# A recurrent block with an FP4 feed-forward gate: stacked half slices, the pointwise product in two parts, and a new order of work

## The reference

```python
xn = _layernorm(x, axis=-1)
s = _L0_attn_ref(xn, ...)      # the recurrent branch
g = _silu(_L0_ffn_ref(xn, w_gate, w_up, w_down))
return x + s * g

# the recurrent branch (weights of 256 x 256, 512 x 256, 1024 x 256, 256 x 1024)
x = causal_dwconv(rmsnorm(x, conv_norm_g), dw_w, dw_b, pw_w, pw_b) + x   # 3 taps, then pointwise
x = min_gru(rmsnorm(x, gru_norm_g), gru_w) + x                           # a scan along the 512 tokens
h = gelu(rmsnorm(x, ff_norm_g) @ ff_w1.T + ff_b1)
x = h @ ff_w2.T + ff_b2 + x

# the FP4 branch: inner size 704, every operand rounded in blocks of 16
gate, up = fp4_linear(x, w_gate), fp4_linear(x, w_up)
h = silu(gate) * up
h = fp4_linear(h, w_down)
# fp4: scale = max|block| / 6, then the nearest of 0, .5, 1, 1.5, 2, 3, 4, 6
```

## Time and profile before

| | |
|---|---|
| Median of 3 runs | 1086.87 us (1084.11 to 1087.17) |
| The profiled execution's own time | 1085.26 us |
| Its span, first to last instruction | 1083.5 us |
| PE busy | 1061.8 us, 98% of the span |
| DVE busy | 934.5 us, 86% |
| ACT busy | 607.3 us, 56% |
| POOL busy | 147.5 us, 14% |
| Granted PE clock, mean | 0.997 |

### The profile page before, as it was taken

How to read it: one execution, slowest core, us unless ns; L and a number is a source line. 1 busy time by engine, 2 the same in 40 slices (tenths; PEclk the granted TensorE clock), 3 DMA queues, 4 the chain that set the end, 5 groups by cost and what they waited for, 6 DMA issues and landing times. The chain is left out here.

```text
span 1083.5 us, 18319 instructions
## 1 busy us (share of the span) xinstructions
PE 1061.8 (98%) x6954; PEld 967.9 (89%) x6954; DVE 934.5 (86%) x1720; ACT 607.3 (56%) x967; POOL 147.5 (14%) x123
## 2 busy tenths in 40 slices
PE   7899999999999999999999999999999999999998
PEld 6788989989898998989999898998989899898998
DVE  6978988989888898988889898898989889898895
ACT  5564464564746547474654747455574645647452
POOL 1230101112020110201111010111101011120010
PEclk9999999999999999999999999999999999999999
DMA  7000001010010101001010010101001010100110
GB/s 248 1 21 1 1 2 59 1 60 1 1 59 1 59 1 47 13 2 59 1 60 1 21 40 1 59 1 60 1 1 59 1 59 1 59 1 2 39 40 21
DMA packets 29365, 31.45 MB, mean 29 GB/s; under 512 B 1120, under 2 KB 28512, under 8 KB 29280
## 3 DMA queue, kind: packets, MB, share of 16 engines
q1 hardware_dynamic: 28448, 29.43, 8.7%
q10 hardware_dynamic: 832, 0.87, 0.2%
HBM read 21.90 MB, written 8.39 MB: 28 GB/s over the span
## 5 line engine op out<-in xcount | busy, mean ns | idle before, releaser
L990 PE MATMUL gu_ps<-gu_hi,xq_hi 128*128 128x352 f32 x512 | 168.3, 329 | 0.0
L990 PE MATMUL gu_ps<-gu_lo,xq_hi 128*128 128x352 f32 x512 | 165.9, 324 | 0.0
L990 PE MATMUL gu_ps<-gu_hi,xq_lo 128*128 128x352 f32 x512 | 165.7, 324 | 0.0
L990 PE MATMUL w_ps<-w_hi,act_hi 128*128 128x256 f32 x480 | 140.1, 292 | 0.0
L990 PE MATMUL w_ps<-w_hi,act_lo 128*128 128x256 f32 x480 | 135.1, 281 | 0.0
L990 PE MATMUL w_ps<-w_lo,act_hi 128*128 128x256 f32 x480 | 134.9, 281 | 0.0
L990 PE MATMUL w_ps<-dn_hi,hqt_hi 128*128 128x256 f32 x384 | 116.6, 304 | 2.0 <-DVE hqt_lo L519 2.0
L990 PE MATMUL w_ps<-dn_hi,hqt_lo 128*128 128x256 f32 x384 | 108.5, 283 | 0.0
L990 PE MATMUL w_ps<-dn_lo,hqt_hi 128*128 128x256 f32 x384 | 108.4, 282 | 0.0
L818 ACT ACTIVATE g<-w_ps 128x256 f32<-128x256 f32 x64 | 24.7, 385 | 147.7 <-PE w_ps L990 147.6
L496 DVE TENSOR_TENSOR hid<-sl,gu_ps 128x704 f32<-128x704 f32 x64 | 56.8, 887 | 58.8 <-PE gu_ps L990 58.2
(11 more groups left out here) (136 smaller groups left out, 2703.6 us busy)
## 6 DMA issues: line engine op xcount, KB each, us to landing
x_in<-x_dram SPq DMA_DIRECT2D x16, 512.0 KB, 5.8
x_res<-x_dram SPq DMA_DIRECT2D x16, 512.0 KB, 5.0
out_dram<-o SPq DMA_DIRECT2D x15, 512.0 KB, 3.5
act<-w_t_dram SPq DMA_DIRECT2D x1, 1024.0 KB, 11.3
w_f<-w_t_dram SPq DMA_DIRECT2D x1, 1024.0 KB, 13.8
w_f<-w_down_dram SPq DMA_DIRECT2D x1, 704.0 KB, 9.4
hid<-w_gate_dram SPq DMA_DIRECT2D x1, 640.0 KB, 5.9
hid<-w_up_dram SPq DMA_DIRECT2D x1, 640.0 KB, 9.3
```

The source lines that it names most:

```text
L990: done = M.matmul(psum, l, r, start=first and i == 0, stop=last and i == len(terms) - 1)
```

## The change

1. Stacked half slice. The 64 padding columns of `hq` are no longer zero: `fp4_hidden_values` writes the half slice's 64 values a second time there, with one more small VectorE instruction. The transposed piece then holds the half slice in both halves of its 128 rows, `dn_hi` and `dn_lo` likewise. `hidden_low` writes the low part of five slices to `hqt_lo`, and the low part of the half slice over the lower 64 rows of `hqt_hi` (a second small instruction, `twin`). One matmul of this piece with `dn_hi` then gives high x high and low x high together, so `down` has 17 matmuls in place of 18.
2. Split pointwise. `pw` becomes `pw_hi` and `pw_lo`, and `y` gets `y_hi` (ScalarE, two casts a chunk, `front_y_high`) and `y_lo` (VectorE, two subtractions a chunk, `front_y_low`). The four fp32 matmuls a chunk become four products of three fp32r matmuls. `y_hi` shares the home of `keep`, and `y_lo` that of `cand`.
3. VectorE's order: the first half of `front_moments` (`front_stats`) moves to the end of the body before, the second half to the middle of the next one, ahead of `gelus_low`, from chunk 2 on; `gelus_low` does 4 + 4 tiles in place of 5 + 3; `front_taps` stands ahead of the rounding; `output(c - 1, 1)` ahead of `scaled_low`.
4. GpSimd's sum waits for the fourth low part of the next chunk in place of the fifth. SyncE's load of x stands ahead of the store.
5. TensorE's order: in the body, the x2b transposes that open an ff2 tile are issued on their own (`ff2_open`), and `front_xc` moves ahead of the last ff2 tile. In the tail the last tile's ff2 stands ahead of its down.
6. `first`: the low parts of the ff weights move from GpSimd to VectorE (`ff_low`), weights 3 to 5 move behind the start of ff1, and the `keep_busy` counts change.

```diff
-        pw = sb("pw", [P, KD, D])
+        pw_hi = sb("pw_hi", [P, KD, D], F32R)
+        pw_lo = sb("pw_lo", [P, KD, D], F32R)
...
+            def fp4_hidden_values(dst, rounded):
+
+                n, last = NBI * FP4_BLOCK, NFULL * P // FP4_BLOCK
+                fp4_values(dst[:, 0:n], NBI, rounded)
+                return V.scalar_tensor_tensor(blocks(dst[:, n:KI * P], NBI - last),
+                                              blocks(q_m[:, NFULL * P:n].bitcast(BF16), NBI - last),
+                                              1.0 / UNIT, spread(q_scale[:, last:NBI], NBI - last),
+                                              ALU.mult, ALU.mult)
...
+            def front_y_low(c):
+
+                for k in range(KD):
+                    dve.wait_ge(yhi_ready, KD * c + k + 1)
+                    V.tensor_tensor(y_lo[:, k, :], y[:, k, :], y_hi[:, k, :].bitcast(F32),
+                                    ALU.subtract).then_inc(ylo_ready, 1)
...
-                V.tensor_tensor(hqt_lo[:], hqt_ps, hqt_hi[:].bitcast(F32), ALU.subtract).then_inc(hqtlo_ready, 1)
+                V.tensor_tensor(hqt_lo[:], hqt_ps[:, 0:NFULL, :], hqt_hi[:, 0:NFULL, :].bitcast(F32), ALU.subtract)
+
+                twin = hqt_hi[LAST:P, NFULL, :]
+                V.tensor_tensor(twin, hqt_ps[LAST:P, NFULL, :], twin.bitcast(F32),
+                                ALU.subtract).then_inc(hqtlo_ready, 1)
...
-                if c < B - 2:
-                    pool.wait_ge(actlo_ready, KF * (c + 1) + 5)
+                pool.wait_ge(actlo_ready, KF * (c + 1) + (4 if c < B - 2 else KF))
...
                 hidden_values(c - 1, 2, fp4_round(NBI, ratios))
-                gelus_low(c - 1, range(5, KF))
+                if front and c > 1:
+                    front_moments(carried["stats"])
+                gelus_low(c - 1, range(4, KF))
                 hidden(c, 2)
...
+            def front_y_high(c):
+
+                for k in range(KD):
+                    act.wait_ge(y_ready, KD * c + k + 1)
+                    act.wait_ge(pw_done, KD * c)
+                    act.wait_ge(x2_ready, KD * c)
+                    A.copy(y_hi[:, k, :], y[:, k, :]).then_inc(yhi_ready, 1)
...
-                for j in range(KF // 2):
+                gelus(c, (0,))
+                if front:
+                    front_y(c + 1)
+                gelus_high(c, (0,))
+                for j in range(1, KF // 2):
                     gelus(c, (j,))
                     gelus_high(c, (j,))
                 if front:
-                    front_y(c + 1)
-                    gelus(c, range(KF // 2, KF))
+                    gelus(c, range(KF // 2, KF - 2))
+                    front_y_high(c + 1)
+                    gelus(c, range(KF - 2, KF))
...
-                        last = product(w_ps[:, e, :], pw[:, k, e * P:(e + 1) * P], y[:, k, :], False, k == KD - 1)
+                        last = product(w_ps[:, e, :], (pw_hi[:, k, e * P:(e + 1) * P], pw_lo[:, k, e * P:(e + 1) * P]),
+                                       (y_hi[:, k, :], y_lo[:, k, :]), False, k == KD - 1)
...
-                for k in range(KI):
-                    last = product(bank[:, 0:D], (hqt_hi[:, k, :], hqt_lo[:, k, :]),
-                                   (dn_hi[:, k, :], dn_lo[:, k, :]), k == 0, k == KI - 1)
-                last.then_inc(dn_done, 1)
+                for k in range(NFULL):
+                    product(bank[:, 0:D], (hqt_hi[:, k, :], hqt_lo[:, k, :]), (dn_hi[:, k, :], dn_lo[:, k, :]),
+                            k == 0, False)
+
+                M.matmul(bank[:, 0:D], hqt_hi[:, NFULL, :], dn_lo[:, NFULL, :], start=False, stop=False)
+                M.matmul(bank[:, 0:D], hqt_hi[:, NFULL, :], dn_hi[:, NFULL, :], start=False,
+                         stop=True).then_inc(dn_done, 1)
...
-                    if t < T - 1:
-                        hq_transposes(c, t + 1, (hqtlo_ready, T * c + t + 1))
-                    ff2(c, t, gu_ps[:, t // 2, t % 2, :], None)
+                for t in range(2, T):
+                    hq_transposes(c, t, (hqtlo_ready, T * c + t))
+                    last_open(t)
+                    last_ff2(t)
+                    pe.wait_ge(g_ready, T * c + t - 1)
+                    down(c, t, w_ps[:, t % 2, :])
```

More of the change, by code:

```diff
@@ L137, in mixed_recurrent_kernel @@
         xs_lo = sb("xs_lo", [P, KD, L], F32R)
-        keep = sb("keep", [P, KD, L])
+        keep, y_hi = shared_home(("keep", [P, KD, L], F32), ("y_hi", [P, KD, L], F32R))
         take = xs
-        cand = sb("cand", [P, KD, L])
+        cand, y_lo = shared_home(("cand", [P, KD, L], F32), ("y_lo", [P, KD, L], F32R))
         y = cand
@@ L611, in _ @@
             carried = {}
             def first():
-                front_moments(0)
+                front_moments(front_stats(0))
+                dve.wait_ge(pwhi_ready, 1)
+                V.tensor_tensor(pw_lo[:], pw_f, pw_hi[:].bitcast(F32), ALU.subtract).then_inc(pwlo_ready, 1)
                 front_rows(0)
-                front_fp4_values(0, front_fp4_ratios(0))
+                rounded = fp4_round(T * NBD, front_fp4_ratios(0))
                 front_taps(0)
-                weight_values(0, weight_ratios(0, weight_scales(0)))
+                front_fp4_values(0, rounded)
@@ L724, in tail @@
                 last_output(0)
+                last_output(1)
                 hidden_low(c, 3)
-                for t in range(1, T):
-                    last_output(t)
+                last_output(2)
+                last_output(3)
             over_chunks(first, body)
@@ L1110, in ff2 @@
                              start=k == 0, stop=False)
+            def ff2(c, t, bank):
+                pe.wait_ge(acthi_ready, KF * (c + 1))
+                pe.wait_ge(actlo_ready, KF * (c + 1))
+                tok = slice(t * P, (t + 1) * P)
                 for j in range(KF):
@@ L1146, in weight_rest @@
                 for i, (hi, bank) in enumerate(places):
-                    last = M.matmul(bank, minus_ident[:], hi, start=False, stop=i == len(places) - 1)
+                    last = M.matmul(bank, minus_ident, hi, start=False, stop=i == len(places) - 1)
                 last.then_inc(wqm_done, 1)
@@ L1173, in down_rest @@
                     n = min(4, KI - k)
-                    last = M.matmul(hqt_ps[:, k:k + n, :], minus_ident[:], dn_hi[:, k:k + n, e * P:(e + 1) * P],
+                    last = M.matmul(hqt_ps[:, k:k + n, :], minus_ident, dn_hi[:, k:k + n, e * P:(e + 1) * P],
                                     start=False, stop=True)
@@ L1261, in body @@
                 spread_scale(c * 2 + 1, gu_ps[:, 0, 1, :], (cand_ready, KD * c + 1))
-                ff2(c - 1, 3, w_ps[:, 3, :], (hqtlo_ready, T * c))
-                ff2(c - 1, 2, w_ps[:, 2, :], (g_ready, T * c))
-                ff1(c, range(KF // 2))
+                ff2_open(c - 1, 3, w_ps[:, 3, :], (hqtlo_ready, T * c))
+                ff2(c - 1, 3, w_ps[:, 3, :])
                 if front:
@@ L1267, in body @@
                     front_xc(c + 1)
+                ff2_open(c - 1, 2, w_ps[:, 2, :], (g_ready, T * c))
+                ff2(c - 1, 2, w_ps[:, 2, :])
+                ff1(c, range(KF // 2))
+                if front:
                     ff1(c, range(KF // 2, KF))
```

260 lines of the change are left out of this document (150 added, 110 removed).

## The result

The changed kernel takes 1088.96 us (median of 20 runs, 1087.33 to 1091.09), the kernel before 1086.86 in the runs beside it (20 runs, 1084.07 to 1089.27). The ratio is 1.0020, 95% interval [1.0012, 1.0029]: 0.2% slower, where I had forecast 1083.4, 0.3% faster. The size lies inside the 0.3% that I called no change, but the interval doesn't hold 1, so the direction was wrong too. The median is 5.6 us above the forecast. Of these, 1.4 are no error of a term: I forecast from a profiled execution, which lay 1.6 under its median, and the profiled one here (1087.56, span 1085.7) lies 1.4 under its own.

A forecast was written before the change was run, and what follows sets the result against it. TensorE (98% busy) was taken to bound the kernel, with VectorE (86%) close behind. Start -5.4, thirteen bodies +4.7 and tail -1.2 gave -1.9 from the profiled 1085.3, so 1083.4 us; range 1080 to 1087, outer 1074 to 1096.

The forecast's parts named there:

- The gross saving: TensorE in a body: four down products save 0.48 and four pointwise products 0.64, together 1.12 us.
- The third down: Second hid to third tile's down: VectorE needs 12.0 us, TensorE arrives after 11.0 and waits 1.0 a body.
- What is left, between nothing and 0.9 ... I take 0.4: Body's end: VectorE's lateness, with GpSimd's sum holding q_wide, after absorption; 0.4 us a body on top of the 1.0.
- E + 11.5: Body's end: E is the start of ff1; the prediction put the start of y_lo at E + 11.4.
- The start: Up to body 2: 5.4 us gained, bounds 3 to 8, with ff1 starting 4.1 earlier.
- 0.8 + 1.2 = 2.0: VectorE's additions ahead of ff1: pw_lo and the wait for its DMA 0.8, y_lo 1.2.
- 3.5 + 5.8 - 2.45 - 0.8 = 6.05: VectorE ahead of ff1: stalls gone 3.0 to 3.5, weights moved 5.8; added ff_low 2.45, idle estimated at 0.8.
- The tail: Last chunk: 1.4 of ff2's wait and 0.4 of matmuls go, last step adds 0.6; net 1.2 us gained.
- The sum is absorbed: Rival: VectorE is free 0.5 us sooner at the body's end; a body takes 63.95, total 1078.7; chance 0.25.
- the third down doesn't wait: Rival: TensorE keeps its 1.0 a body, 13 us less, total 1066; chance 0.05.
- The clock rival: Rival: 1.4 us of idle in a body halves TensorE's clock, costing 1.6 a body; total 1104; chance 0.12.
- Small instructions dear: Rival: VectorE's small instructions cost 0.43 each, adding 0.6 to 0.8 a body; total 1092; chance 0.18.

The follow-up runs named there:

- kernel with four places: Changed kernel with statistics and moments moved, GpSimd's sum at VectorE's taps, five gelu low parts first, x2b transposes of tile 3 ahead of second spread: 1062.99 us.
- plain pointwise kernel: Changed kernel with the split of the pointwise product alone undone (pw and y in plain fp32, no y_hi or y_lo): 1090.00 us, ratio 1.0038.
- refilled kernel: Changed kernel with the statistics moved ahead of y_lo and the moments ahead of the recurrence, where VectorE was idle: 1074.71 us.

## Why the prediction was wrong, step by step

**The gross saving** is right: products 0.23 apart, 17 matmuls a down, and with no wait left a body costs 62.74. That is 1.24 under the kernel before, for 1.12 gross and the root's wait of 0.22, which is gone there too.

**The third down** is right in place and size. The way there was forecast at 12.0 and is 12.01. From the second down to the third it takes 0.95 us more than in the kernel with four places, where I had 1.0. That it fits to 0.01 is luck: up to its end the low part in two instructions takes 1.06 for 0.89, 0.17 more and not 0.08, and I left out that `hid` now starts 0.08 ahead of the last low part's end. In a row, where the next instruction's start counts, the second instruction costs 0.29 (1.16 for 0.87), where I had 0.08 too.

**"What is left, between nothing and 0.9 ... I take 0.4"** is the step that failed in the bodies. By the terms in front of it 0.3 + 0.8 late less 0.37 + 0.2 absorbed leave 0.5, and I wrote 0.4 without a reason. `q_wide` lost 0.76, and at the second down this costs TensorE 0.56: cutting the sum down or moving it away gave 0.57 both. So a body is 62.74 + 0.95 + 0.56, and 0.25 for the root as what is left to 64.50. With 0.4 in place of 0.56 it would be 64.34, and the forecast had 64.33. Thirteen times 0.16 is 2.1, the 2.0 us by which that term came out worse. (A slip without effect: `y_lo` is at E + 11.5 by my own numbers, not 11.4; the trace has it at 672.83 - 661.68 = 11.15.) I had also named no place for it; the wait stands ahead of the second down, and I had looked for it only at `hid`.

**The start** gave 4.3 for 5.4. ff1 began at 55.98, 3.15 earlier for 4.1, and that is where the missing us lies. VectorE's timeline cuts the stretch at the first sum of squares: here, then in the kernel before, then in the plain pointwise kernel.

```profile
27.78 0.69 DVE L545 TENSOR_TENSOR xs<-xs 128x512 f32<-128x512 f32 x1 [0.18 <-ACT xs L837]
```
```profile
25.83 0.69 DVE L524 TENSOR_TENSOR xs<-xs 128x512 f32<-128x512 f32 x1 [1.20 <-ACT xs L779]
```
```profile
27.98 0.69 DVE L544 TENSOR_TENSOR xs<-xs 128x512 f32<-128x512 f32 x1 [2.75 <-ACT xs L832]
```

Ahead of it 1.95 us are lost, where I had 0.8 + 1.2 = 2.0, but not for my reasons. `y_lo` took 2.36 for the 1.2 that I had, beside GpSimd's low part of the gru weights; I had counted the two such blocks that go (of the kind of the earlier trace rows), not the one that comes. By the same section of the Trainium skill a VectorE instruction with two SBUF inputs contends with a GpSimd instruction that reads SBUF; `y_lo` is one, and the trace agrees. I had used that page for `hid` alone. But this block delays nothing: the plain pointwise kernel has no `y_lo`, waits 2.75 us for ScalarE's squares instead, and starts ff1 at 56.18, no earlier. The squares themselves come late. TensorE's transposes of xq, with the pointwise product behind them in its list, wait for `xq`, which VectorE now writes behind the taps (point 3 of the change). Here, and in the kernel before:

```profile
20.00 1.09 PE L1074 MATMUL gu_ps<-ident,xq 128*128 128x128 f32 x8 [1.69 <-DVE xq L427]
```
```profile
16.44 1.09 PE L1002 MATMUL gu_ps<-ident,xq 128*128 128x128 f32 x8 [0.44 <-DVE xq L427]
```

This is read from the traces; no run puts that order back. Behind the squares 28.20 us pass to ff1 for 33.30 before, 5.1 gained where my terms give 3.5 + 5.8 - 2.45 - 0.8 = 6.05. The term that failed is the last, VectorE's idle, "I estimate, 0.8". It is 0.35 + 0.84 + 0.15 + 0.49 = 1.83, in a stretch where the kernel before lists none:

```profile
33.46 1.29 DVE L560 TENSOR_TENSOR xs<-w_ps,x 128x512 f32<-128x512 f32 x2 [0.35 <-PE w_ps L1126]
...
41.12 0.69 DVE L572 SCALAR_TENSOR_TENSOR cand<-gu_ps,cand 128x512 f32<-128x512 f32 x1 [0.84 <-ACT cand L887]
...
50.33 0.69 DVE L550 TENSOR_REDUCE ss_sum<-gu_ps 128x4 f32<-128x512 f32 x1 [0.15 <-PE gu_ps L1118]
...
53.17 1.29 DVE L560 TENSOR_TENSOR xs<-gu_ps,x 128x512 f32<-128x512 f32 x2 [0.49 <-PE gu_ps L1126]
```

**The tail** gave 0.2 for 1.2. The order is worth 1.9 against the kernel before (54.7 for 56.7 to the end), more than I took. But the diff also moves the last sum into the tail (the `else KF` in the diff, which point 4 of the change leaves unsaid), and my term doesn't mention it; there it holds `q_wide` for 1.74 us, and the second down waits 1.11 behind it:

```profile
1062.10 1.74 DVE L403 TENSOR_SCALAR q_wide<-q_amax 128x44 f32<-128x44 f32 x1
```
```profile
1065.60 0.36 PE L1062 MATMUL w_ps<-dn_hi,hqt_hi 128*128 128x256 f32 x1 [1.11 <-DVE hqt_hi L539]
```

That costs 1.44 by the run with the sum at its old time. Of the 0.5 left, 0.3 goes ahead of the last body's first scan, which comes 27.26 us into that body for 26.98.

**The rivals.** "The sum is absorbed" is refuted, "the third down doesn't wait" too. The clock rival is refuted: from 164 to 1002 us the granted clock is 1.00, with idle pieces of 0.30 and 0.83 in each body. "Small instructions dear" comes nearest to what happened: not by the upper end of each, but they are enough to turn the half slices into a loss. Undone, they make the changed kernel 0.8%, some 8 us, faster. Whether the split product pays here isn't settled: undone, a body takes 64.63 for 64.50, but the ratios 1.0038 and 1.0020 have intervals that overlap.

All three terms missed towards slower, and the chances with them: I gave 0.23 to slower and 0.48 to faster, though my own reading had used up VectorE's reserve and the change gives it 49 us of work. In the bodies and the tail the cause is the same, GpSimd's sum beside `q_wide`, sized too low in one and missing in the other; at the start it is VectorE's idle time.

## What to carry to other kernels

When the second engine gets the work that the first one saves, its idle places matter more than its busy share: here the same instructions gave 1.002 or 0.979 of the old time, by four places in two lists and one wait. Ahead of a change, list every stretch in which GpSimd runs and which VectorE instructions will stand beside it; here the ones that read PSUM were the place for it. A block counts only where VectorE isn't about to wait anyway: at the start 1.07 us of it cost nothing. And reckon each stretch from the last point at which the leading engine released it: a saving upstream of that point is lost, as the plain pointwise product showed.

## What the runs showed of the hardware

VectorE instructions with one input in PSUM (`hid`, 0.88; the taps, 0.75) kept their time beside GpSimd's sum, and so did a reduction from SBUF (`q_amax`, 0.88). `q_wide`, one SBUF input of 44 columns, was held until the sum ended (0.95 to 1.74 us for 0.19). Two-input `y_lo` took 2.36 for 1.29 beside GpSimd's low part of the gru weights, which itself took 3.49, for 2.50 in the refilled kernel, where it runs beside the write of `xq` and ends ahead of `y_lo`. There the write of `xq` is the one held, 2.11 for 1.22: it also has two SBUF inputs.

The granted clock went to 0.50, TensorE's lower level of 1.2 GHz, after 2.13 us of idle in one tail and, in the kernel before, after 1.96 and 1.97 us at the start. It stayed at 1.00 after 1.74, after 1.11, and also after 2.91 us at the start of the refilled kernel (20.96 us). So the length of the idle piece alone doesn't tell, in these traces, whether the clock falls.
